# A macaron block on one core: keys and queries stacked over 98 and 96 rows, values in their own step

## The reference

```python
def _L0_attn_ref(x, Wqkv, bqkv, Wo, bo):
    kqv = (x @ Wqkv + bqkv).reshape(b, s, 3, NUM_HEADS, HEAD_SIZE)
    q, k, v = kqv[:, :, 0], kqv[:, :, 1], kqv[:, :, 2]
    scores = jnp.einsum('bsnh,btnh->bnst', k, q) / math.sqrt(HEAD_SIZE)
    scores = jnp.triu(scores) + -10000.0 * jnp.tril(ones, k=-1)
    attn = jax.nn.softmax(scores, axis=2)
    out = jnp.einsum('bnkq,bknh->bqnh', attn, v)
    return out.reshape(b, s, NUM_HEADS * HEAD_SIZE) @ Wo + bo
...
x = x + 0.5 * _L0_ffn_ref(_layernorm(x, axis=-1), L0_ffn_weight, L0_ffn_bias)
x = x + _L0_attn_ref(_layernorm(x, axis=-1), L0_attn_Wqkv, L0_attn_bqkv, L0_attn_Wo, L0_attn_bo)
x = x + 0.5 * _L0_ffn_ref(_layernorm(x, axis=-1), L0_ffn_weight, L0_ffn_bias)
```

## Time and profile before

| | before |
|---|---|
| median of 3 runs | 1117.07 us (1115.98 to 1118.72) |
| the profiled execution | 1115.44 us, span of its trace 1113.7 us |
| PE busy | 1067.9 us, 9472 matmuls |
| ACT busy | 921.7 us |
| DVE busy | 738.9 us |
| POOL busy | 344.0 us |
| mean granted clock of PE | 0.983 of full speed |

### The profile page before, as it was taken

One profiled execution on the slowest core, in us unless ns is written; L12 is line 12 of the kernel. 1 busy time (PEld: TensorE's weight loads), 2 busy tenths in 40 slices (PEclk: granted clock), 3 DMA queues, 4 the chain that ended last, 5 costly groups with the idle time before them and its releaser, 6 DMA issues.

```text
span 1113.7 us, 26124 instructions
## 1 busy us (share of the span) xinstructions
PE 1067.9 (96%) x9472; PEld 691.1 (62%) x9472; DVE 738.9 (66%) x2306; ACT 921.7 (83%) x2577; POOL 344.0 (31%) x471
## 2 busy tenths in 40 slices
PE   5799999999999999999999999999999999999896
PEld 3576656565666565665666666675666666665465
DVE  6866577787535767789644766789744667765344
ACT  2269998999989989889988988878988998999641
POOL 3841232233001313345201322435401322311343
PEclk8898999999999999999999999999999999998999
DMA  6463211021004110421112211421112212000121
GB/s 207 153 217 125 97 50 40 3 78 50 24 19 154 32 59 31 158 73 43 38 41 87 77 59 50 144 78 40 51 40 86 69 40 69 21 12 13 60 66 38
DMA packets 42015, 77.71 MB, mean 70 GB/s; under 512 B 5536, under 2 KB 11680, under 8 KB 41888
## 3 DMA queue, kind: packets, MB, share of 16 engines
q1 hardware_dynamic: 41888, 76.04, 20.5%
HBM read 49.81 MB, written 25.17 MB: 67 GB/s over the span
## 4 chain that ended last, share of the span: by engine, by line
PE 76%; ACT 11%; DVE 6%; issue 2%; POOL 2%; DMA 1%; SPq 0%; DVEq 0%; ACTq 0%; POOLq 0%
PE bank L1173 31%; PE bank L1294 10%; PE bank L1232 10%; PE bank L1266 10%; PE bank L1195 7%; ACT masked_scores L1073 6%; ACT prob L1099 4%; PE bank L1184 3%; PE bank L1274 3%; DVE masked_scores L909 2%; DVE st L859 1%; DMA xt<-in_L_attn_x_dram 1%; DVE hn L878 1%; POOL xt L769 1%; PE bank L1251 1%
## 5 line engine op out<-in xcount | busy, mean ns | idle before, releaser
L909 DVE CUSTOM_DVE_ANT_0 masked_scores<-bank,mask 128x512 f32<-128x512 f32 (+3 forms) x768 | 379.6, 554 | 221.3 <-PE bank L1232 220.2
L1073 ACT ACTIVATE masked_scores<-masked_scores,mst 128x512 f32<-128x512 f32 (+3 forms) x768 | 467.7, 620 | 2.9 <-DVE mst L909 2.9
L1099 ACT ACTIVATE prob<-bank 128x512 f32<-128x512 f32 (+1 forms) x640 | 302.0, 559 | 58.5 <-PE bank L1274 57.4
L1173 PE MATMUL bank<-hT,wqk 128*128 128x512 f32 x768 | 190.9, 397 | 0.0
L808 POOL TENSOR_SCALAR_AFFINE_SELECT prob<-prob 128x512 f32<-128x512 f32 (+1 forms) x96 | 78.6, 819 | 346.5 <-ACT prob L1099 345.8
L1266 PE MATMUL bank<-qT,kT 32*128 32x512 f32 (+2 forms) x2304 | 169.6, 378 | 4.5 <-DVE kT L886 1.6
L1232 PEld LDWEIGHTS bank<-kT,qT 32*128 32x128 f32 x2304 | 94.4, 185 | 115.6 <-issue 52.8
L1232 PE MATMUL bank<-kT,qT 32*128 32x512 f32 (+2 forms) x2304 | 161.2, 377 | 3.4 <-ACT prob L1099 2.6
L1173 PEld LDWEIGHTS bank<-hT,wqk 128*128 128x128 f32 x768 | 140.4, 188 | 37.9 <-ACT prob L1099 8.2
L1073 ACT ACTIVATION_READ_ACCUMULATOR masked_scores<-masked_scores,mst 128x1 f32 x768 | 156.4, 204 | 0.0
L1266 PEld LDWEIGHTS bank<-qT,kT 32*128 32x128 f32 x2304 | 97.7, 185 | 70.4 <-issue 48.4
(11 more groups left out here) (87 smaller groups left out, 971.7 us busy)
## 6 DMA issues: line engine op xcount, KB each, us to landing
wqk<-weight_scratch SPq DMA_DIRECT2D x30, 512.0 KB, 3.4
wvo<-weight_scratch SPq DMA_DIRECT2D x20, 512.0 KB, 6.0
xt<-in_L_attn_x_dram SPq DMA_DIRECT2D x32, 256.0 KB, 4.2
residual_scratch<-xt SPq DMA_DIRECT2D x32, 256.0 KB, 2.0
xt<-residual_scratch SPq DMA_DIRECT2D x32, 256.0 KB, 3.1
out_dram<-xt SPq DMA_DIRECT2D x32, 256.0 KB, 2.0
o<-in_L_attn_Wqkv_dram SPq DMA_DIRECT2D x12, 256.0 KB, 4.7
weight_scratch<-o SPq DMA_DIRECT2D x6, 512.0 KB, 3.0
```

The source lines that it names most:

```text
L909: nc.vector.tensor_tensor_reduce(masked_scores[:, h, at:at + n], psum(u, h)[:, at:at + n], mask[:, off:off + n], -SCALE, BIG, ALU.add, ALU ...
L1073: nc.scalar.activation(of, of, ACT.Exp, bias=mst[:, c + kc, to:to + 1], scale=-1.0, accum_out=ssum[:, c + kc, to:to + 1]).then_inc(a_free, 1)
L1099: nc.scalar.activation(prob[:, at % 2, h, off:CW], psum(("S", b, n), h)[:, off:CW], ACT.Exp, scale=SCALE)\
L1173: m = nc.tensor.matmul(psum(u), left(x, k), right(y, k), start=(n == 0), stop=(n == len(terms) - 1))
```

## The change

Keys and queries are **stacked**. A projection piece is evacuated by ACT and DVE into one staging tile `stage` (high and low part, heads at their 32 rows). Then SP issues 12 DMAs (`stack`), three parts by four heads, each of 32 rows and 512 columns of 4 bytes: a key piece becomes `kst[n]` with the rows high, low, high under each other and one column block per head, a query piece `qst[n]` with high, high, low. So one matmul over 96 rows holds all three terms of a head. Rows 96 and 97 of the keys are ones, those of the queries the maxima (`rows` writes them there), and the scores matmul runs over 98 rows. Scores are 4 matmuls a step in place of 16, or 8 in place of 32, maxima 4 or 8 in place of 12 or 24. Each matmul, or last of a head's two, signals its head.

There are three buffers for keys and three for queries (`NPIECE`). `outlived` says which step must have read the old piece first; `MOVES` places each stack in a slot, and SP waits there for `ring_free` of the piece and for `s_full` of that step. `stage` is single: ACT's `high` of a `P` waits until the piece before is stacked (`stacked`). The maxima's row tile is single too and waits for its previous transfer.

PE's order in a slot is now: scores, block, small uses, products, values of the same step. The exponentials wait head by head, and the sum of the previous block's head 3 stands between heads 1 and 2. `prob` has 6 head tiles in place of 8, `masked_scores` 2 in place of 4: DVE's maximum of head 2 waits for ACT's sum of head 0 of the same block. The mask is split in two where its heads wrap around. In the table `P` moves from slots 0, 1, 2, 9 of a group mostly to slots 1, 2, 8, 9, and `F`, `T`, `V` move by a slot here and there.

```diff
 def pieces(b, g):
-    second = (Q_, K_) if g == 0 else (K_, Q_)
-    return [("P", b, g, K_, 0), ("P", b, g, Q_, 0)] + [("P", b, g, j, 1) for j in second]
+    return [("P", b, g, K_, 0), ("P", b, g, Q_, 0), ("P", b, g, Q_, 1), ("P", b, g, K_, 1)]
...
 GROUP1_ROWS = (
-    "C T3.3 P | A | X3.6",
+    "C T3.3 F2.2 | A | X3.6",
     "N M F2.3 P | A | X3.7",
...
+def piece(u):
+    n = 2 * (u[1] * GROUPS + u[2]) + u[4]
+    return n % NPIECE, n // NPIECE + 1
+def outlived(u):
+    n = 2 * (u[1] * GROUPS + u[2]) + u[4] - NPIECE
+    if n < 0:
+        return None
+    last = (6, 9) if u[3] == K_ else (2, 9)
+    return n // 2 * STEPS + last[n % 2]
+SLOT_OF = {s.b * NSTEP + s.step: k for k, s in enumerate(SLOTS) if s.step is not None}
+MOVES = [[] for _ in SLOTS]
+for at, s in enumerate(SLOTS):
+    for u in s.uses():
+        if u[0] == "P":
+            old = outlived(u)
+            MOVES[at + 1 if old is None else max(at + 1, SLOT_OF[old])].append(u)
+assert [u for moves in MOVES for u in moves] == PROJECTIONS
...
+        kst = [sb(f"kst{n}", [P, 4, CW], F32R) for n in range(NPIECE)]
+        qst = [sb(f"qst{n}", [P, 4, CW], F32R) for n in range(NPIECE)]
+        stage = sb("stage", [P, 2, CW], F32R)
+        prob = sb("prob", [P, NPROB, CW])
...
+            def stack(u):
+                sp.wait_ge(ring_free, freed(u))
+                if outlived(u) is not None:
+                    sp.wait_ge(s_full, 4 * outlived(u) + 4)
+                n, _ = piece(u)
+                to, parts = (kst[n], (HI, LO, HI)) if u[3] == K_ else (qst[n], (HI, HI, LO))
+                for j, part in enumerate(parts):
+                    for h in range(4):
+                        sp.dma_start(to[HD * j:HD * j + HD, h, :].bitcast(F32), stage[HD * h:HD * h + HD, part, :].bitcast(F32))\
+                            .then_inc((kst_in if u[3] == K_ else qst_in)[n], 16)
...
-                dve.wait_ge(ring_full, full(u))
                 for h in range(4):
-                    if EARLIER[u] is not None:
-                        dve.wait_ge(a_free, block_at(EARLIER[u], h))
+                    dve.wait_ge(ring_full, full(u) - 3 + h)
+                    if h >= 2:
+                        dve.wait_ge(a_free, block_at(u, h - 2))
+                    elif EARLIER[u] is not None:
+                        dve.wait_ge(a_free, block_at(EARLIER[u], h + 2))
                     for j, r, at, n, off in block_tiles(u):
                         to = 4 * h + r
-                        nc.vector.tensor_tensor_reduce(masked_scores[:, h, at:at + n], psum(u, h)[:, at:at + n],
+                        nc.vector.tensor_tensor_reduce(masked_scores[:, h % 2, at:at + n], psum(u, h)[:, at:at + n],
                                                        mask[:, off:off + n], -SCALE, BIG, ALU.add, ALU.min,
...
+                    at = PROJECTIONS.index(u)
+                    if at:
+                        act.wait_ge(*stacked(PROJECTIONS[at - 1]))
+                    i = nc.scalar.activation(stage[:, HI, :], psum(u), ACT.Identity, bias=bias_of(u[3], u[2]))
...
-            def exponentials(b, n):
+            def exponentials(b, n, heads):
                 off = live(n % STEPS)
                 at = step(b, n)
-                for h in range(4):
-                    nc.scalar.activation(prob[:, at % 2, h, off:CW], psum(("S", b, n), h)[:, off:CW], ACT.Exp, scale=SCALE)\
+                for h in heads:
+                    act.wait_ge(s_full, 4 * at + h + 1)
+                    if 4 * at + h >= NPROB:
+                        act.wait_ge(value_done, (4 * at + h - NPROB) // 4 + 1)
+                    nc.scalar.activation(prob[:, place(at, h), off:CW], psum(("S", b, n), h)[:, off:CW], ACT.Exp, scale=SCALE)\
                         .then_inc(s_exp, 1)
             for k, s in enumerate(SLOTS):
                 b = s.b
                 if s.step is not None:
-                    act.wait_ge(s_full, step(b, s.step) + 1)
-                    if step(b, s.step) >= 2:
-                        act.wait_ge(value_done, step(b, s.step) - 1)
-                    exponentials(b, s.step)
+                    exponentials(b, s.step, (0, 1))
                 if k and SLOTS[k - 1].blocks:
                     block_sums(SLOTS[k - 1].blocks[-1], (3,))
+                if s.step is not None:
+                    exponentials(b, s.step, (2, 3))
...
-                    if kc:
-                        pe.wait_ge(ring_free, freed(("P", b, g, K_, kc)))
-                    for term, (x, y) in enumerate(((HI, HI), (LO, HI), (HI, LO))):
+                    pe.wait_ge(*stacked(("P", b, g, Q_, c)))
+                    pe.wait_ge(*stacked(("P", b, g, K_, kc)))
+                    for h in range(4):
+                        bank_free(u, h)
                         for j, r, at, keys, _ in block_tiles(u):
                             n = max(HALF, keys)
-                            for h in range(4):
-                                if term == 0 and j == 0:
-                                    bank_free(u, h)
-                                row = slice(HD * h, HD * h + HD)
-                                m = nc.tensor.matmul(psum(u, h)[:, at:at + n], query_piece(b, g, c)[row, x, P * r:P * r + P],
-                                                     kT[g % 2][row, y, CW * kc:CW * kc + n], start=(term == 0 and j == 0),
-                                                     stop=(term == 2 and j == len(u[5]) - 1))
-                    m.then_inc(ring_full, 1)
+                            m = nc.tensor.matmul(psum(u, h)[:, at:at + n], queries_of(b, g, c)[0:STACK, h, P * r:P * r + P],
+                                                 keys_of(b, g, kc)[0:STACK, h, 0:n], start=(j == 0), stop=(j == len(u[5]) - 1))
+                        m.then_inc(ring_full, 1)
...
-                for term, (x, y) in enumerate(((HI, HI), (LO, HI), (HI, LO))):
-                    for kb, off, at in parts:
-                        for h in range(4):
-                            if term == 0 and kb == keys[0]:
-                                bank_free(u, h)
-                            row = slice(HD * h, HD * h + HD)
-                            nc.tensor.matmul(psum(u, h)[:, at:at + CW - off], kT[g % 2][row, x, P * kb:P * kb + P],
-                                             query_piece(b, g, c)[row, y, off:CW], start=(term == 0 and kb == keys[0]),
-                                             stop=False)
                 if keys[0] == 0:
                     pe.wait_ge(mrow_in[c], 32 * group(b, g))
-                for kb, off, at in parts:
-                    for h in range(4):
-                        row = slice(HD * h, HD * h + 2)
-                        m = nc.tensor.matmul(psum(u, h)[:, at:at + CW - off], onesr[row, :], mneg[row, c, off:CW],
-                                             start=False, stop=(kb == keys[-1]))
-                m.then_inc(s_full, 1)
+                for h in range(4):
+                    bank_free(u, h)
+                    for kb, off, at in parts:
+                        key = P * (kb % QPC)
+                        m = nc.tensor.matmul(psum(u, h)[:, at:at + CW - off], keys_of(b, g, kb // QPC)[0:ROWS, h, key:key + P],
+                                             queries_of(b, g, c)[0:ROWS, h, off:CW], start=(kb == keys[0]), stop=(kb == keys[-1]))
+                    m.then_inc(s_full, 1)
...
             for s in SLOTS:
                 b, n = s.b, s.step
-                if b == B and s.row == 0:
-                    values(B - 1, NSTEP - 1)
                 if n is not None:
                     scores(b, n)
-                if n is not None and step(b, n):
-                    done = (b, n - 1) if n else (b - 1, NSTEP - 1)
-                    values(*done)
                 for u in s.uses():
                     use(u)
+                if n is not None:
+                    values(b, n)
```

163 lines of the change are left out of this document (87 added, 76 removed).

## The result

| | before | after |
|---|---|---|
| median of 4 runs | 1117.88 us (1115.98 to 1118.72) | 1445.45 us (1440.03 to 1451.70) |
| span of the profiled execution | 1113.7 us | 1438.3 us |
| mean granted clock of TensorE | 0.983 | 0.887 |

The ratio is 1.2935, with an interval of 1.2871 to 1.2999. The forecast was 1215 with a range of 1130 to 1290: the direction was right, and the time lies 155 us above the upper end. Times are medians; one execution of the run with the three moves together fell into a slower state of this chip (clock 0.547, 1803.6 us) and is left out of its median.

A forecast was written before the change was run, and what follows sets the result against it. PE was taken as the bound, busy 1067.9 of 1113.7 us without a gap in its steady slots. The terms summed as 1115.4 - 52 + 75 + 27 + 51 = 1216; forecast 1215 us, range 1130 to 1290.

The forecast's parts named there:

- edit 4: Stacking by 12 DMAs per piece on SP: ACT waits at the single staging tile, PE behind it, +51 us.
- edit 3: New table: 19 slots without a product, 14 before, bounded by exponentials, mask and values: +27 us (0 to +40).
- the head: Start of the kernel: four pieces follow one another with maxima behind them, +10 us.
- The issue: Stacking DMAs on SP: 0.40 us from one to the next, bounds 0.35 and 0.58.
- The slack: ACT stands some 2.4 us in 21 places; PE feels it less about 0.8 of slack, 34 us.
- The queries: Query piece stacked at T+16.4, its maxima due at T+15.9: 0.5 us a group, 7 us.
- Rival (b): Stacking on SP rules, with an issue near 0.55 us: +150 for +51, 1315 us; chance 0.12.
- Edit 1: Stacked matmuls: scores -34 us, maxima +2, products behind full maxima -20; together -52, between -25 and -75.
- Edit 2: Values at the end of their own step: second and third uses wait for exponentials, net +75 us (+40 to +110).
- Other edits: 0: Two masked-score buffers, six probability tiles, ones and rows in shared tiles: put at 0.
- What waits behind the stacks on SP: Loads of x and weights and the maxima's row transfers, needed a slot or more later: costed at nothing.
- Rival (e): Waits let PE's clock fall; a tenth of the time at 1.2 GHz costs some 50 us more, 1265; chance 0.05.

The follow-up runs named there:

- the run with the three moves together: Kernel before with values at the end of their own step, the split order on ScalarE and two masked-score tiles, no stacking: 1318.00 us.
- the DRAM kernel: Changed kernel with each staging tile written to DRAM by one transfer and read back by three, nothing left out: 1311.85 us.
- the last stacked run: Changed kernel with one stacking transfer per piece from the fourth on, values one step later, four exponentials in a row, four 16-bit masked-score tiles: 1146.22 us.
- the run with one transfer: Changed kernel with only one of 12 stacking DMAs per piece from the fourth key and query piece on, so scores are stale: 1247.23 us.
- the one with 12 transfers: Changed kernel with all 12 transfers, but values one step later, four exponentials in a row and four 16-bit masked-score tiles: 1368.80 us.

## Why the prediction was wrong

One path from the changed kernel to the kernel before, by medians:

| step undone | us | forecast |
|---|---|---|
| 11 of 12 stacking issues | 1445.5 to 1247.2: 198 | 34 + 7 of edit 4 |
| values at the end of their own step | to 1199.9: 47 | 75, with the split order; 27 of edit 3 |
| split order, two masked tiles | to 1146.2: 54 | in the 75; 0 |
| the rest, to 1117: the head | 30 | 10 of edit 4 |
| the rest: stacked matmuls in the steady part | -1 | -52 |

Another order of steps gives somewhat other amounts (223 for 198), but no other picture.

**Edit 4 is the step that failed**, 227 us for 51. Its mechanism is there as written: ACT waits at the staging tile and PE behind it. Three terms of it were mis-sized, and a fourth, the head: there the four pieces follow one another, 10 us forecast and 29.6 measured. (1) The issue. The prediction took 0.40 us from one to the next. SP's row of 0.326 in the earlier trace rows belongs to a store to DRAM, and its row of 0.540 to a transfer from SBUF to SBUF. I held the length of the runs for what told them apart; a quarter of the length changed nothing in the issues. The issues in the changed kernel, and those of the transfer from the staging tile to DRAM in the DRAM kernel:

```profile
L725 SPq DMA_DIRECT2D kst<-stage x384: 512/590/1652, 61.7 to 1336.7; - x192
```

```profile
L724 SPq DMA_DIRECT2D stack_scratch<-stage x64: 370/382/1067, 61.2 to 1198.0; - x64
```

An instruction takes 0.590, and from one to the next it is 0.62 (7.49 / 12), above even the high end of 0.58. The row of the same kind, 0.540, was in my hands, and I chose between the two by a guess. The tile is free 9.0 us after its release, where T+2.1 to T+8.5 gave 6.4. (2) The slack. I gave PE 0.8 us less to wait than ACT and 21 places. It was 29 places for ACT with 5.6 us each (162.3 / 29) and 27 for PE with 4.5 (122.1 / 27). What I had missed is that the full projection occupies a bank of the ring; the slack is the work up to that bank, and what ACT does late afterwards is late too. (3) The queries. 0.5 us a group, 7 in all, was a difference of two large numbers, and with the issue at 0.62 it became 34.0 us of waits in 17 places, beside the two in the head. Rival (b), for an issue near 0.55, gave the right sign of this and 1315, with a chance of 0.12; it had the price of stacking at 150, and 223 was found. That SP's issues would rule was among the rivals; the cost does not grow evenly with their length, though, but from a knee, and the issue time lay on the far side of it.

**Edit 1 was half right.** It is read in the last stacked run, from the first scores to the last, from the start of each block to the start of the next. Scores and their maxima row fell from 200 to 166 us, the 34 of the forecast, but half by luck: undisturbed blocks gained 0.13, 0.12 and 0.10 us for the forecast 0.24, 0.22 and 0.11, some 19 us, and the rest came from blocks that had been held up in the kernel before. Products fell from 331 to 317, for a forecast of 20. What ate both is the maxima, from 145 to 183 where 2 were forecast: 1.05 us for 512 columns and not 0.91, 1.12 ahead of a `C`, and 9.6 us of waits for exponentials (2.7 before). Values and the other uses make up the rest, some 9 us.

The rows above tell when a full block is dear. In the changed kernel the scores at 701.25, behind values, take 1.05, and in the last stacked run the scores ahead of values 1.02 and the maxima behind values 1.05. Maxima of 512 columns behind scores take 0.93 in the changed kernel (the median of its undisturbed blocks). So a full block costs what was forecast only between full blocks; a tiled block beside it adds about 0.1. Blocks of 12 products show the same: 2.94 between two tiled blocks (kernel before), 2.83 between maxima and values (changed kernel), 2.74 between two full blocks (last stacked run). In the earlier trace rows I had put all of the 0.2 down to the maxima ahead of the products; half belongs to the scores behind them. The values are tiled and stay tiled, so in both orders this change of form only moved: to both sides of the values. The Trainium skill (TensorEngine Tiling, Key Properties) says that a change of tiling mode drains TensorE; this trace agrees, with 0.1 us for each side of a full block.

**Edit 2 was right in kind, and its size was in part luck.** 47 us for the values and 21 for the split order are 68, for the 75 forecast. But the 75 were waits of products and small uses for exponentials in some 106 slots. In the run with one transfer PE waits for them in 59 places, 24.8 us in all. About as much of the 47 is the values' wait for the mask, which belongs to edit 3. For the kernel before the same argument would have been too low, 109 + 39.

**Edit 3 was right in kind.** Its bound for a slot without a product, exponentials, mask and values in a row, is the wait for the mask: 21.8 us in 14 places, for 27 forecast in 19 slots. It holds only with the values in their own step. With them a step later 0.7 us of it is left, and with everything else undone the steady part has the length of before. So the amount stands in the row of the values and not in that of the table.

**"Other edits: 0" fell.** I compared times within a block and forgot that DVE has other work behind the block, which PE needs as well. The two masked tiles cost 61 us alone in the kernel before. The six probability tiles were never undone: in the last stacked run ACT waits 35.9 us in 79 places for values, with the steady part as long as before, so no cost of theirs is seen there, and with the values in their own step it was not tested. What waits behind the stacks on SP, put at nothing as well, does not appear among the waits of PE in the changed kernel.

**Rival (e), the clock**, is part of all of it. The changed kernel and the last stacked run execute the same 5632 matmuls. The first has PE busy for 1172.3 us at a granted clock of 0.887, the second for 1058.8 at 0.969. That is 113 us more busy time for the same work. The levels are 1.2 and 2.4 GHz, and by the granted clock in the traces PE was busy at the lower one for 255 us in the first and for 54 in the second (35 in the kernel before). The clean pair is the one with 12 transfers and with one, all three moves undone: of the 224 us between their spans 139 are idle time of PE and 86 busy time. Every wait listed above has thus a second price, and the amounts of the table hold it. Stretches show the same: 1.00 in the one without gaps, 0.91 in the one with 28 us of them. The Trainium skill (TensorE: Matmul & The Clock Gate, What's actually happening) lets the clock follow how busy TensorE has recently been; the trace agrees, with 0.887 at a busy share of 82% and 0.969 at 93%. What share of the 328 us the clock itself makes can be bounded by an estimate: 220 us more at half speed than before cost at most half, 110 us. It is an upper end, since a matmul that waits on operands counts as busy too and loses less. The rival had 50 us for it and a chance of 0.05; its mechanism is in every row of the table.

**What was to show it.** ACT's copy waiting for DMA was there, in 29 places, for 5.6 us each and not 2 to 3. So were exponentials that PE waits for, but half a microsecond each in 44 places of the changed kernel, and not in most slots. PE's share is 82%, not 88. The 12 issues take 7.5 us, not 5. "A stacked matmul that costs other than 0.23" was among what would make the prediction wrong, and it did: 0.26.

## What to carry to other kernels

Before a buffer is filled by many small transfers, price the issue from a row of the same kind (memory to memory), multiply by their number, and compare the product with the distance to the next piece: below it an issue was cheap here (8 us for the whole kernel), beyond it dear (26). Where banks go round in a ring, a result that nobody can empty stops the matrix engine as soon as the ring comes back to its bank, so its slack is counted in banks and not in time. And where an engine has no gap, an edit that couples two others is not to be put at nothing (39 to 109 us here): ask what stands behind the waiting instruction on its own engine, beyond the block in question.

## What had not been expected of the hardware

- A transfer from SBUF to SBUF takes SP 0.59 us to issue, and 12 take 7.5 us with 64 KB as with 16 KB each; one from SBUF to DRAM takes 0.38 with 512 KB and 0.33 with 256 KB. It may be the memory or the shape (32 rows for 128); the runs do not separate them.
- Four full matmuls of 512 columns beside column-tiled values take 1.02 to 1.05 us, between full blocks 0.93; 12 full products take 2.94, 2.83 and 2.74 with a tiled block on both sides, on one and on none. In the last stacked run the first weight load of maxima starts only as the tiled block ends, and this idle of the load engine has no releaser in the profile. That the load is what costs the 0.1 was not tested.
- A wait of PE was paid more than once: with 139 us more idle time came 86 us more busy time, at a mean clock of 0.887 for 0.969.
- Of three causes that each hold up another engine (109, 39 and 61 us) nearly the whole sum was found, 200 of 209. With an engine that had no gap the waits hardly hid one another.
